# Second attention: chunks turned over three passes instead of two, score tiles in rising rows, masks in two passes

## The reference

```python
q = (x @ Wq.T); k = (x @ Wk.T); v = (x @ Wv.T)       # 32 heads of 32, 8 key heads, rope on q and k
draft = einsum('bhqd,bhkd->bhqk', qr, kr) + causal    # causal: finfo.min above the diagonal
_, idx = top_k(draft, 128)                            # num_remain = max(min(1024, 128), 1024 - 921)
mask = full(neg); mask[idx] = 0; mask = where(causal_future, neg, mask)
out = softmax(draft / sqrt(32) + mask) @ v @ Wo.T
```

## Time and profile before

| | us |
|---|---|
| runs, median of 3 | 5083.04 |
| the profiled execution, outside its trace | 5084.22 |
| span of its trace | 5082.4 |
| TensorE, VectorE, ScalarE, GpSimd busy | 4031.7, 3263.8, 2811.0, 317.3 |
| second attention: first count to the last move of a chunk | 2190.1 to 4757.3 |

### The profile page before, as it was taken

The page is one execution under the profiler, slowest core; times in us unless marked ns, Lnnn a source line. Parts: engine busy times, 40 slices in busy tenths (PEclk is TensorE's granted clock), DMA queues, the critical chain, the costliest instruction groups (busy, mean ns, idle before and its releaser), DMA issues. The chain is left out here.

```text
span 5082.4 us, 84318 instructions
## 1 busy us (share of the span) xinstructions
PE 4031.7 (79%) x25752; PEld 2300.6 (45%) x25752; DVE 3263.8 (64%) x9571; ACT 2811.0 (55%) x6546; POOL 317.3 (6%) x1173
## 2 busy tenths in 40 slices
PE   6998999999999999926676367677677677676899
PEld 2445766666444444413343244343344344343454
DVE  3555777776333345568778777778777778776244
ACT  1114777776000011168888488888888888887101
POOL 1000000000000000000110011010110110111000
PEclk9999999999999999967877687777777777786899
DMA  3335323233111123311011101111001111010442
GB/s 140 77 71 159 79 59 76 61 73 102 51 50 50 46 52 76 87 30 24 5 27 27 23 5 27 27 27 25 21 11 28 27 26 25 11 22 4 123 116 78
DMA packets 308431, 260.30 MB, mean 51 GB/s; under 512 B 188672, under 2 KB 242704, under 8 KB 307920
## 3 DMA queue, kind: packets, MB, share of 16 engines
q1 hardware_dynamic: 307376, 254.32, 19.7%
q0 software_dynamic: 544, 0.07, 0.0%
HBM read 176.21 MB, written 78.12 MB: 50 GB/s over the span
## 5 line engine op out<-in xcount | busy, mean ns | idle before, releaser
L1069 ACT ACTIVATE a_sign<-arena,a_state 128x384 fp8e4<-128x384 f32 (+5 forms) x1056 | 917.8, 871 | 99.1 <-DVE a_state L1276 59.9
L967 PE MATMUL a_ps_s<-k,q 128*128 128x512 bf16 (+3 forms) x1536 | 453.3, 432 | 619.1 <-DVE arena L1339 410.1
L1038 ACT ACTIVATE a_probT<-a_ps_t 128x512 f32<-128x512 f32 (+3 forms) x768 | 365.7, 483 | 324.5 <-PE a_ps_t L986 264.8
L967 PEld LDWEIGHTS a_ps_s<-k,q 128*128 128x128 bf16 x1536 | 147.8, 119 | 833.6 <-DVE arena L1339 474.7
L979 PE MATMUL a_ps_t<-ident,arena 128*128 128x128 f32 x1584 | 334.9, 328 | 203.3 <-ACT a_probT L1038 167.6
L1069 ACT ACTIVATE a_sign<-a_third,a_state 128x384 fp8e4<-128x384 f32 (+2 forms) x480 | 417.2, 871 | 79.1 <-DVE a_state L1276 76.2
L738 ACT ACTIVATE a_prob<-a_x_neg,a_shift 128x640 f32<-128x640 f32 (+7 forms) x512 | 397.1, 776 | 87.7 <-DVE a_x_neg L781 62.2
L781 DVE TENSOR_SCALAR_CACHE_REDUCE a_x_neg<-a_ps_s 128x640 f32<-128x640 f32 (+7 forms) x512 | 378.8, 751 | 41.2 <-PE a_ps_s L662 25.4
L1287 DVE MAX8 a_nine<-a_below 128x8 f32<-128x256 f32 (+6 forms) x448 | 371.1, 828 | 34.5 <-issue 1.8
L677 PE MATMUL a_ps_t<-ident,a_prob 128*128 128x128 f32 x2304 | 364.6, 282 | 35.3 <-issue 15.4
L1005 PE MATMUL a_ps_o<-a_probT,vals 128*64 128x128 f32 x4608 | 368.4, 302 | 0.0
(11 more groups left out here) (263 smaller groups left out, 6905.5 us busy)
## 6 DMA issues: line engine op xcount, KB each, us to landing
q<-qk SPq DMA_DIRECT2D x256, 256.0 KB, 4.6
qk<-p_qkT SPq DMA_DIRECT2D x32, 960.0 KB, 6.2
h_rows<-h SPq DMA_DIRECT2D x32, 512.0 KB, 6.9
k<-qk SPq DMA_DIRECT2D x256, 64.0 KB, 5.0
h<-tok_h SPq DMA_DIRECT2D x16, 512.0 KB, 4.0
arena<-in_wo SPq DMA_DIRECT2D x16, 512.0 KB, 6.3
o<-a_o SPq DMA_DIRECT2D x16, 512.0 KB, 2.7
q<-o SPq DMA_DIRECT2D x16, 512.0 KB, 5.6
```

The costliest lines, as they stand in the source:

```text
L967: nc.tensor.matmul(ps_s[:, n % 2, a:a + w], q[:, y, head, i * P:(i + 1) * P], k[:, y, a:a + w], start=(y == 0), stop=False, skip_group_che ...
L1038: nc.scalar.activation(probT[:, n % 4, 0:w], ps_t[:, (n + 1) % 2, 0:w], ACT.Exp).then_inc(probT_ready, 1)
L1069: ins = nc.scalar.activation(to, xs[mine][:, at:at + w], ACT.Sign, scale=-1.0, saturate=False, bias=state[:, par, 0, n:n + 1], accum_out=s ...
```

## The change

```diff
+    RISING = [(m, i) for i in range(TT) for m in range(2)]
...
+        EARLY, FIRST, HALF = 16, 6, 6
+        half_turned = 2 + max(n for n, m, i, a, w in CH if i < HALF)
...
                     def scores(n):
-                        m, i = TILES[n]
+                        m, i = RISING[n]
...
                         for n in range(0, NC, 2):
+                            if EARLY <= n < EARLY + FIRST and st["score"]:
+                                scores(n - EARLY)
+                                scores(n - EARLY + 1)
                             turn(*CH[n])
                             turn(*CH[n + 1])
...
-                        for n in range(2 * TT):
+                        for n in range(FIRST if st["value"] else 0, 2 * TT):
                             scores(n)
...
-                    EVAC_PASSES, BETWEEN = 2, 40
-                    counted = [sum(2 + i for _, i in (RANKED * EVAC_PASSES)[:k] if i > 1) + BETWEEN * (k // NS)
...
+                    EVAC_PASSES, LEFT = 3, 2
+                    PER = NC // EVAC_PASSES
+                    counted = [sum(2 + i for _, i in RANKED[:n] if i > 1) for n in range(NS + 1)]
+                    spread = [next(n for n in range(NS) if counted[n + 1] * (PER - LEFT) >= (c + 1) * counted[NS])
+                              for c in range(PER - LEFT)] + [NS - 1] * LEFT
+                    after = [p * NS + n for p in range(EVAC_PASSES) for n in spread]
...
-                        if p == 2 and st["keep"]:
+                        if p == EVAC_PASSES and st["keep"]:
                             top_evac()
...
-                    KEEPS = [(), (), range(0, TT - 1), range(TT - 1, NS - 2), range(NS - 2, NS)]
-                    FETCHES = [(), (), range(0, 4), range(4, 12), range(12, 2 * TT)]
-                    GATHERS = [(), (), (), range(0, 3), range(3, NS - 4)]
+                    by_row = [RANKED.index(r) for r in RISING if r[1]]
+                    KEEPS = [(), (), by_row[:2 * HALF - 2], by_row[2 * HALF - 2:], ()]
+                    FETCHES = [(), (), range(0, FIRST), range(FIRST, 12), range(12, 2 * TT)]
+                    GATHERS = [(), (), (), by_row[0:4], by_row[4:NS - 4]]
...
-                        if p == 2 and st["value"]:
-                            dve.wait_ge(turn_done, (s - 2) * TURNED + TURNED)
+                        if p in (2, 3) and st["value"]:
+                            dve.wait_ge(turn_done, (s - 2) * TURNED + (half_turned if p == 2 else TURNED))
...
-                            if st["value"]:
-                                output()
                         elif p > 2:
-                            for k in range(max(len(keeps), len(fetches))):
...
+                            for r in keeps:
+                                mark(r).then_inc(mask_ready, 1)
+                            for k, n in enumerate(fetches):
+                                fetch(n)
+                                for g in share(gathers, k, len(fetches)):
+                                    gather(g, y)
+                        if p == 3 and st["value"]:
+                            output()
```

More of the change, by code:

```diff
@@ L1042, in top_evac @@
                         nc.scalar.copy(topT[:, :], ps_t[0:SPLITS * 2 * TT, 0, 0:P]).then_inc(probT_ready, 1)
-                    EVAC_PASSES, BETWEEN = 2, 40
-                    counted = [sum(2 + i for _, i in (RANKED * EVAC_PASSES)[:k] if i > 1) + BETWEEN * (k // NS)
-                               for k in range(EVAC_PASSES * NS + 1)]
-                    moved = [sum(c[4] for c in CH[:k]) for k in range(NC)]
-                    after = [sum(f * moved[-1] < g * counted[-1] for f in counted[1:]) for g in moved]
+                    EVAC_PASSES, LEFT = 3, 2
[4 more added lines that the diff above has]
+                    after = [p * NS + n for p in range(EVAC_PASSES) for n in spread]
                     def evacs(step):
@@ L1054, in evacs @@
                             for k, c in enumerate(CH):
-                                if min(after[k], EVAC_PASSES * NS - 1) == step:
+                                if after[k] == step:
                                     evac(*c)
@@ L1339, in fetch @@
                         nc.vector.tensor_scalar(new_x[:, at:at + w], ps_s[:, n % 2, 0:w], 1.0, None, ALU.mult, ALU.max,
-                                                accum_out=top[:, n:n + 1]).then_inc(x_ready, 1)
+                                                accum_out=top[:, m * TT + i:m * TT + i + 1]).then_inc(x_ready, 1)
                     def output():
@@ L1404, in part @@
                             dve.drain()
-                            if st["value"]:
-                                output()
                         elif p > 2:
-                            for k in range(max(len(keeps), len(fetches))):
-                                if k == len(keeps):
-                                    dve.drain()
-                                for r in keeps[k:k + 1]:
-                                    mark(r).then_inc(mask_ready, 1)
-                                for n in fetches[k:k + 1]:
-                                    fetch(n)
-                                for n in share(gathers, k, 4) if k < 4 else ():
-                                    gather(n, y)
+                            for r in keeps:
[6 more added lines that the diff above has]
+                            output()
                         if p == 4:
@@ L1419, in part @@
                         if p == 4 and st["score"]:
-                            for n in range(NS - 4, NS):
+                            for n in by_row[NS - 4:]:
                                 gather(n, y)
@@ L1425, in slot @@
                         part(p)
-                        if p == 2 and isinstance(s, int) and s == PAIRS + 1:
+                        if p == 3 and isinstance(s, int) and s == PAIRS + 1:
                             scale_first()
```

## The result

The changed kernel takes 5007.6 us (median of four runs, 5001.7 to 5014.9), against 5083.8 of the kernel before on the same chip: ratio 0.9846, 95% interval 0.9834 to 0.9858. The forecast was 5038, faster; the range held the time, but the gain is 76 us where 45 were forecast. The profiled execution took 5014.9 us, the longest of the four.

The account below looks back on a forecast made before the run. No engine was full; the loop between counts and guesses bound the kernel. Terms of -1.4 us a slot over 29 slots (-41), with -4, -6, +7 and -1, gave -45: 5038 us, own range 4998 to 5076, full range 4915 to 5115.

Parts of the forecast that it names:

- three loop heads: VectorE's stops of 2.86 us at the head of a loop round, formerly hidden under the moves, show in three slots: +7.
- Pass 0: Eight chunk moves in and behind it instead of fourteen: 15.5 us against a mean of 21.4, -5.9 a slot.
- Pass 1: Counting, five moves and the wait for the guess: 15.4 us against 16.8, -1.4 a slot.
- Pass 2 without the clock: Five moves lengthen counting to 12.9; VectorE's guess starts 1.3 late: 16.5 us against 12.9, +3.6 a slot.
- The clock in the chain: TensorE enters pass 2's chain of turns and scores at 1.2 GHz in most slots, for 5 us: +2.8 a slot.
- Pass 3: ScalarE unchanged; VectorE runs over if scores come slowly at the low clock: +0.8 a slot.
- Pass 4: VectorE, the late one, has less work and is about 0.6 late at the low clock: -1.3 a slot.
- Slot 31: It has no scores and so no chain in pass 2: -4.
- Behind it: In slot 32 the masks wait for chunk 15, no longer 23, and only four remain: -6.
- The clock is kept: Rival: TensorE keeps its clock in pass 2's chain, -4.2 to -5.5 a slot, 4919 us; chance 0.22.
- The clock stays low through the chain: Rival: TensorE stays low until scores 4 and 5, +4.8 a slot, slower, 5102 to 5218 us; chance 0.18.
- only the lump moves: Rival: VectorE's passes 2 and 3 each end 2 us later, using up the gain, 5083 us; chance 0.10.

Follow-up runs that it names:

- spread_only: Kernel before with only ScalarE's moves spread over three passes; scores, masks and output copy stay where they were: 5336.3 us, ratio 1.0495.
- check_first: Changed kernel with pass 2's check for failing rows ahead of the fetches of scores 4 and 5 on VectorE: 4969.3 us, ratio 0.977.
- no_early_scores: Changed kernel with no scores between the turns; all twelve tiles computed behind the last products and fetched in pass 3: 5033.2 us, ratio 0.9895.
- changed_again: The changed kernel, nothing edited, timed once more: 5006.5 us, ratio 0.9841.
- fill: Changed kernel plus unread bf16 matmuls, fourteen after turns 0 and 1, four after the products of chunks 0 to 12: 4977.9 us, ratio 0.9789.
- turn_fill: Changed kernel plus unread fp32 identity transposes, twenty after turns 0 and 1, six after the products of chunks 0 to 12: 4981.2 us, ratio 0.9791.

## Why the prediction was right, and where not

The sign, the places and most terms held; the sum was -1.4 us a slot (and +7 for three loop heads, together -34 us in 29 slots), measured -66.6. That 5007.6 lies in the forecast's own range (4998 to 5076) is in part luck: the clock was charged 49 us too much, and passes 0 and 4 gave 18 us less than forecast.

- *Pass 0*: -5.9 forecast, -5.4 measured, the loop heads' 7 us included, which showed as said: their pass 1 starts 6.0 to 6.3 us after the last count, elsewhere 3.3 to 4.0. In slot 17 it took 15.4, forecast 15.5; VectorE's guess was ready 15.1 us into the pass (forecast 14.9), at 3516.8, and the last move let pass 1 start at 3517.1; in slots that are at the low clock throughout pass 0, the two last moves end 0.5 us later still. spread_only shows that the new table alone does this.
- *Pass 1*: -1.4 forecast, -1.5 measured.
- *Pass 2 without the clock*: 16.5 forecast, 16.7 in slot 17. The split was right too: ScalarE's 2.3 for five moves (counting 10.7 to 12.9), and VectorE 1.3 late by the sum, 1.4 in slot 17, with much the same wait behind the last count in nearly every slot. check_first shows that it is the check behind late scores, and no_early_scores that it goes with them. The last fetch of slot 17 ended 11.4 us after the last count of pass 1 (3540.9, and 3517.1 + 12.4), forecast 10.7.
- *The clock in the chain* is the term that was mis-sized: +2.8 forecast, some +1.1 measured (13.97 of counting against 12.9). The mechanism was right, a chain entered at 1.2 GHz whose moves wait for turns. Two things were off. It happens in 18 of 27 slots and not in nearly all; and where it does, counting takes 14.5, so it costs 1.6 in pass 2 and not 2.8, as part of the low stretch falls into pass 1 (clock 0.91 in 18.2 us of slot 11: 2 x 0.09 x 18.2 = 3.3 us low inside pass 2, where I took 5), and the turns lost there delay only ScalarE's moves: VectorE stays 1.4 late behind a last count that is itself later. This term is 1.7 x 29 = 49 us, more than the whole difference of 32 between -34 and -66.6; pass 0 (0.3 us a slot, the loop heads counted in the forecast) and pass 4 (0.35) take back those 18 us.
- *Pass 3*: +0.8 forecast, +0.6 measured; as forecast it is scores that come slower at the low clock, for at 1.00 the pass takes 12.9 to 13.0. *Pass 4*: -1.3 forecast, -0.9 measured: VectorE is still the later one, by 1.14 us of ScalarE's waiting in slot 17.
- *Slot 31*: -4 forecast, -0.5 measured: pass 0 gave 4.3 and pass 1 0.7, but pass 2 took 4.5 more; it too was at the low clock where pass 2 begins, with 14.7 us of counting there. *Slots 0 and 1*: -1 forecast, what comes ahead of slot 2 took 2.1 more here and 0.9 less in changed_again. *Behind it*: -6 forecast, -4.4 measured. The first turn of slot 33 came 44.2 us after slot 31 instead of 47.7, and waited for the outputs, which I had not seen as the last releaser there:

```profile
4651.12 0.45 PE L982 MATMUL a_ps_t<-ident,arena 128*128 128x128 f32 x1 [4.94 <-DVE a_o L1354]
```

- *The signs.* Of those that were to show the forecast right, two came: pass 1 16.0 us after pass 0, and masks that run past the last count. The guess of pass 2 was to come over 5 us after the last count and came 3.8 after it; the clock in pass 2 was to be under 0.9 and is 0.94 in the mean; and ScalarE still waits before pass 0. The first two of these misses are again the clock's loss, half of which falls into pass 1 and the rest into the counting of pass 2, not behind it.
- *Rivals.* "The clock is kept" is true of a third of the slots, and there its -4.2 to -5.5 us a slot was right where nothing else disturbed: slots 15, 17, 19, 23 and 27 take 72.0 us, -4.6 against 76.6. As a price for the whole kernel 4919 is not shown: fill, with pass 2 at 1.00 in all slots, takes 4978. Its mean slot is 73.1 and not the 71.1 that -5.5 gives; pass 2 is 17.1 with the added work, and pass 3 stays at 13.5, since the clock there is still lost in 21 slots. VectorE's lateness in pass 2 was in the rival's price and doesn't explain the difference. "The clock stays low through the chain" and "only the lump moves" didn't occur. The rule of the Trainium skill, "TensorE: Matmul & The Clock Gate", Part 4: PE-mode transpose, that transposes don't count as busy in the way that other matmuls do, was weighed in the second of them; turn_fill speaks against it for keeping the clock (1.00 in pass 2 of all 27 slots, 4981 us), as far as fp32 transposes between other matmuls go, and leaves it possible for raising it. Pass 1 in the earlier trace rows, nearly all turns and products at 1.00, spoke against it already.

Open: why two slots with nearly the same work differ in the clock at the end of pass 1. What the trace shows is where it came up before: in 16 slots later than 16 us into the slot, and all 16 are low in pass 2; in 11 slots by 14.2 us, and two of them are. In changed_again it is 11 of 12 and 6 of 15, so that doesn't settle it, and no run isolates the cause.

## What to carry to other kernels

When a lump of work that waits for a chain is spread out, ask what else waited for the chain's end: here the spreading alone cost 248 us, the masks in two passes turned that into a gain (0.9895 of before), and the early scores added half a point. In a pass that closes on a hand-over, put what needs late data last and what doesn't into the wait for it, and move work only into a part whose own end something else hides. Price a low clock by who waits for the slowed engine, and for how many of the rounds.

## Of the hardware, not expected

- Four matmuls that nobody reads, behind the products of each pair of chunks from 0 to 13, kept TensorE at 2.4 GHz where it had gone to 1.2: pass 2 was at 1.00 in 27 of 27 slots instead of 9, with or without more such work at the slot's head, and it was worth some 29 us of 5008.
- fp32 transposes of the same duration kept the clock as well as bf16 matmuls did (pass 2 at 1.00 in 27 of 27 slots, counting 13.1 and 13.3 us), though in 8 of 24 slots they brought it up later, at 14.5 to 14.8 us.
- VectorE's stop at the head of a round of the loop, 2.86 us, can be shifted out of sight or into it by a change elsewhere: it cost about 2.4 us in each of three slots here (18.1 us of pass 0 against 15.7 in the mean of the others), and nothing visible before. The row of the changed kernel, head of slot 16:

```profile
3430.18 0.48 DVE L1213 SCALAR_TENSOR_TENSOR a_sign<-arena,a_state,a_two 128x256 fp8e4<-128x256 f32 x1 [3.02 <-issue]
```
